# Sigmoid of the gated experts through the hyperbolic tangent, in a two-layer transformer kernel on one core

## The reference

```python
def _forward(x, ...):
    x1 = jnp.einsum('btd,hd->bth', x, sw1) + sb1
    x2 = jnp.einsum('btd,hd->bth', x, sw2) + sb2
    sh = _ln(jax.nn.silu(x1) * x2, s_ln_g, s_ln_b)            # every token
    shared_out = jnp.einsum('bth,dh->btd', sh, sw3) + sb3
    ...
    h1 = jnp.einsum('md,ehd->meh', x_moe, ew1) + eb1
    h2 = jnp.einsum('md,ehd->meh', x_moe, ew2) + eb2
    z = _ln(jax.nn.silu(h1) * h2, sel_ln_g, sel_ln_b)         # 512 chosen tokens
    out_all = jnp.einsum('meh,edh->med', z, ew3) + eb3
    ...
```

## Time and profile before

| | before |
|---|---|
| median of 3 runs | 1099.81 us (1099.57 to 1100.39) |
| the profiled execution, its own time | 1103.98 us |
| its span in the trace | 1101.8 us |
| busy: PE, DVE, ACT, POOL | 810.7, 722.0, 367.8, 383.9 us |
| TensorE clock granted, mean of the span | 0.91 of full speed |
| chain that ended last, by engine | PE 34%, DVE 29%, issue 13%, ACT 9%, POOL 9% |

### The profile page before, as it was taken

One profiled execution on the slowest core, in us unless ns is written; L12 is line 12 of the kernel. 1 busy time (PEld: TensorE's weight loads), 2 busy tenths in 40 slices (PEclk: granted clock), 3 DMA queues, 4 the chain that ended last, 5 costly groups with the idle time before them and its releaser, 6 DMA issues.

```text
span 1101.8 us, 27848 instructions
## 1 busy us (share of the span) xinstructions
PE 810.7 (74%) x10046; PEld 567.4 (51%) x10047; DVE 722.0 (66%) x1986; ACT 367.8 (33%) x752; POOL 383.9 (35%) x642
## 2 busy tenths in 40 slices
PE   2455527888898888988898888885777777773486
PEld 2344326556666655665666666563444454442364
DVE  4799764565766667565665656664767676675566
ACT  3333313333342433424243342532232423321110
POOL 3566421424233332433324243332232323313322
PEclk9986558999999999999999999997999999995588
DMA  5644300000000000000000000003121211111200
GB/s 214 229 161 170 126 1 1 3 0 0 0 0 0 0 0 0 0 0 0 0 0 0 0 0 1 11 15 97 32 63 32 64 32 64 41 50 39 78 1 5
DMA packets 22250, 42.17 MB, mean 38 GB/s; under 512 B 3341, under 2 KB 17815, under 8 KB 21321
## 3 DMA queue, kind: packets, MB, share of 16 engines
q1 hardware_dynamic: 21512, 40.01, 10.9%
q0 software_dynamic: 704, 1.71, 0.5%
HBM read 33.19 MB, written 8.91 MB: 38 GB/s over the span
## 4 chain that ended last, share of the span: by engine, by line
PE 34%; DVE 29%; issue 13%; ACT 9%; POOL 9%; DMA 2%; POOLq 2%; SPq 0%; DVEq 0%; ACTq 0%
DVE mx L1261 8%; PE ps L385 7%; POOL rs L1625 3%; PE ps L552 3%; PE ps L535 3%; DVE hl L1303 2%; PE ps L594 2%; PE ps L391 2%; PE ps L590 2%; PE ps L589 2%; ACT pT L907 2%; ACT hh L847 2%; PE ps L483 1%; PE ps L587 1%; PE ps L392 1%
## 5 line engine op out<-in xcount | busy, mean ns | idle before, releaser
L1623 POOL TENSOR_TENSOR rs<-mv,cst 128x1 f32<-128x1 f32 x164 | 35.8, 219 | 589.5 <-DVE mv L1061 529.4
L1261 DVE TENSOR_REDUCE mx<-ps 128x16 f32<-128x2048 f32 x48 | 109.4, 2280 | 0.0
L847 ACT CAST xh<-ps 128x256 bf16<-128x256 f32 x48 | 17.9, 372 | 264.7 <-PE ps L385 264.7
L1625 POOL TENSOR_TENSOR rs<-rs,cst 128x1 f32<-128x1 f32 x164 | 90.8, 554 | 12.8
L907 ACT ACTIVATE pT<-ps 128x1024 f32<-128x1024 f32 x96 | 93.4, 1030 | 2.1 <-PE ps L535 2.1
L391 PE MATMUL ps<-w_hi,hh 128*128 (+1 forms) x272 | 74.8, 275 | 7.5 <-DVE hl L1303 5.7
L552 PE MATMUL ps<-pT,v 128*32 128x128 f32 x1536 | 58.1, 285 | 24.1 <-ACT pT L907 24.1
L535 PE MATMUL ps<-qh,khm 32*128 32x128 bf16 x768 | 45.0, 222 | 41.8 <-issue 34.6
L847 ACT COPY mT<-ps 128x128 bf16<-128x128 bf16 x48 | 12.8, 266 | 187.7 <-PE ps L514 187.7
L392 PE MATMUL ps<-w_hi,hl 128*128 (+1 forms) x272 | 74.6, 274 | 0.0
L393 PE MATMUL ps<-w_lo,hh 128*128 (+1 forms) x272 | 74.6, 274 | 0.0
(11 more groups left out here) (338 smaller groups left out, 2675.4 us busy)
## 6 DMA issues: line engine op xcount, KB each, us to landing
stage<-in_w SPq DMA_DIRECT2D x16, 768.0 KB, 5.2
vec<-in_vec SPq DMA_DIRECT2D x4, 1152.0 KB, 7.6
vec<-in_tw SPq DMA_DIRECT2D x16, 216.0 KB, 2.6
ctxc<-in_ctx SPq DMA_DIRECT2D x20, 128.0 KB, 2.3
comb<-x SPq DMA_DIRECT2D x16, 128.0 KB, 2.1
comb<-t SPq DMA_DIRECT2D x16, 128.0 KB, 2.0
shared<-x1b SPq DMA_DIRECT2D x16, 128.0 KB, 1.7
out<-x SPq DMA_DIRECT2D x16, 128.0 KB, 1.8
```

The lines of the kernel that those rows point to most:

```text
L847: return nc.scalar.copy(dst, src)
L1261: nc.vector.tensor_reduce(mx[:, :], att.rearrange("p g s k -> p (g s) k"), AX.X, ALU.max, negate=True).then_inc(m_max, 1)
L1625: tt(rs[:, i, :], rs[:, i, :], halves, ALU.pow).then_inc(done, 1)
```

## The change

In both places where silu is computed, ACT applies Tanh to half of the argument in place of Exp to its negative, and DVE computes (tanh + 1) * a with one scalar_tensor_tensor in place of an addition, a reciprocal and a product. The factor 0.5 that is then missing goes into the product with the other half of the hidden tile, which becomes a scalar_tensor_tensor as well. (sigmoid(a) = (tanh(a/2) + 1)/2.) Two semaphores (`s_e1`, `s_r`) and two waits per block go with the operations.

```diff
             def sh_e(f):
                 act.wait_ge(s_hb, f + C1)
-                A(de[:, 0:HM], h[:, 0:HM], ACT.Exp, scale=-1.0).then_inc(s_e, 1)
+                A(de[:, 0:HM], h[:, 0:HM], ACT.Tanh, scale=0.5).then_inc(s_e, 1)
...
             def hidden_exp(t):
...
-                A(de[:, HM * (t % 2):HM * (t % 2) + HM], ps[:, t % 2, 0:HM], ACT.Exp, scale=-1.0).then_inc(d_e, 1)
+                A(de[:, HM * (t % 2):HM * (t % 2) + HM], ps[:, t % 2, 0:HM], ACT.Tanh, scale=0.5).then_inc(d_e, 1)
...
             def sh_gated(f):
                 dve.wait_ge(s_e, f + C1)
-                ts(de[:, HM:2 * HM], de[:, 0:HM], 1.0, None, ALU.add).then_inc(s_e1, 1)
-                dve.wait_ge(s_e1, f + C1)
-                nc.vector.reciprocal(de[:, 0:HM], de[:, HM:2 * HM]).then_inc(s_r, 1)
-                dve.wait_ge(s_r, f + C1)
-                tt(h[:, 2 * HM:3 * HM], h[:, 0:HM], de[:, 0:HM], ALU.mult).then_inc(s_a, 1)
+                stt(h[:, 2 * HM:3 * HM], de[:, 0:HM], 1.0, h[:, 0:HM], ALU.add, ALU.mult).then_inc(s_a, 1)
                 dve.wait_ge(s_a, f + C1)
-                tt(h[:, 3 * HM:4 * HM], h[:, 2 * HM:3 * HM], h[:, HM:2 * HM], ALU.mult).then_inc(s_g, 1)
+                stt(h[:, 3 * HM:4 * HM], h[:, 2 * HM:3 * HM], 0.5, h[:, HM:2 * HM], ALU.mult, ALU.mult).then_inc(s_g, 1)
...
             def gated(t):
...
-                link(ts(h[:, 0:HM], de[:, HM * (t % 2):HM * (t % 2) + HM], 1.0, None, ALU.add))
-                link(nc.vector.reciprocal(h[:, HM:2 * HM], h[:, 0:HM]))
-                link(tt(h[:, 0:HM], h12[:, 0:HM], h[:, HM:2 * HM], ALU.mult))
-                link(tt(h[:, 2 * HM:3 * HM], h[:, 0:HM], h12[:, HM:2 * HM], ALU.mult))
+                link(stt(h[:, 0:HM], de[:, HM * (t % 2):HM * (t % 2) + HM], 1.0, h12[:, 0:HM], ALU.add, ALU.mult))
+                link(stt(h[:, 2 * HM:3 * HM], h[:, 0:HM], 0.5, h12[:, HM:2 * HM], ALU.mult, ALU.mult))
```

## The result

The changed kernel takes **1083.99 us** (median of 4 runs, 1082.29 to 1084.76), the kernel before 1100.1 in the same comparison: 16.1 us less. The ratio, worked out over the single runs, is 0.9847, 95% interval 0.9826 to 0.9867, which is 16.8 us. Forecast were 1085.4 us and a gain of 14.4. A second comparison, with more runs, gave 1083.57 us after 1102.25 (18.7 us less) and a ratio of 0.984 (0.9822 to 0.9857), which is 17.6 us.

What follows compares the result with a forecast made beforehand. The prediction took stage C for a loop of waits, bound by no engine. Gains of 9.5 (blocks 1 to 13), 2.4 (blocks 14 and 15) and 2.5 (final stage), 14.4 us off 1099.8, gave 1085.4 us, range 1082 to 1088.

Steps and rivals of the forecast that it cites:

- the room of 0.74 us a block: Stage C: PE's projections let t1's transposes start at most 0.74 us earlier a block, of 1.22 saved on DVE.
- Rival A: Stage C: PE's projections don't hold the transposes, so all 1.22 us a block pass on; 20.8 us less, 1079.0; chance 7%.
- rival B: Stage C, blocks 1 to 13: another wait of nearly the same length leaves no gain; only 4.9 us, 1094.9; chance 7%.
- the gain of blocks 1 to 13: Stage C: twelve blocks gain 0.74 us each and block 1 gains 0.59, together 9.5 us.
- I count no change: PE's clock: low stretches counted as unchanged, with 2 us more to 5 us less to be expected.
- rival C: PE's clock in stage C and final stage turns beyond the forecast, likely in favour: 19.4 us less, 1080.4; chance 14%.
- Price of the two operations: DVE: the two new scalar_tensor_tensor cost 0.33 us each with the hand-over, 0.66 together; upper end 0.76.
- Blocks 14 and 15: End of stage C: no projections stand in the way, so both pass on all 1.22 us, 2.4 us together.
- Final stage: Gated operations of tiles 0 and 3 gain 1.25 and 1.23 us, 2.5 together; tiles 1 and 2 nothing.
- Tanh for Exp at nothing: ACT: Tanh takes as long as Exp and comes from the same loaded table, so no change.
- Rival D: ACT: Tanh is not in the loaded table, so loads are added; 24 us slower, 1123; chance 4%.
- The cost of profiling: The profiled execution's 4.2 us above the runs' median were taken as profiling cost; the gain was taken off the median.

Runs made afterwards that it cites:

- one_more: The changed kernel with one more scalar_tensor_tensor of 128x128 on DVE in stage C's shared layer, its result unused: 1082.72 us, ratio 0.9832.
- root_first: The changed kernel with the attention's root ahead of the gated one on POOL, and sh_sum behind sh_y on DVE: 1082.1 us, ratio 0.9828.
- v_behind: The changed kernel with projection_v moved behind the transposes of t1 on PE: 1077.83 us, ratio 0.9795.
- before_again: The kernel before, unchanged, run once more for a second trace: 1101.44 us, ratio 1.0002.
- t1_first_old_ops: The kernel before with the attention's root first on POOL, sh_sum behind sh_y on DVE, t1's transposes ahead of both projections on PE: 1077.96 us, ratio 0.978.

## Why the prediction was right, and where it was not

- *The bound, and the room of 0.74 us a block*: right to the hundredth up to the transposes, and so are the 0.59 of block 1 (8.28 us from `maxima` to the transposes before, 7.69 after). `one_more` (nothing lost), `root_first` (nothing gained) and `v_behind` (0.45 gained) show that PE's order holds them now. Rival A (1079.0) is excluded by the 16.53 us, rival B (1094.9) too.
- *The term that was mis-sized* is the gain of blocks 1 to 13: 12.4 us for 9.5. Of the 2.9, 13 x 0.06 = 0.8 came from behind the start of the transposes, where xh follows 0.07 us sooner when they needn't wait. The rest is the step "I count no change" on the clock: three low stretches, 2.15 us (2.0 in the prediction, which counts block 1 from 17.33 and not from 17.18), went, and went in every trace. The prediction had these 2 us inside its range, as a part of what might come, and gave rival C, which takes the final stage along, 14%; its reason (PE has shorter gaps) fits the traces. The stage C part of C happened, the final stage's part in some executions only, and C's 1080.4 as a whole did not.
- *Price of the two operations*: 0.63 us with their hand-overs in stage C, 0.66 forecast, and 0.66 in the final stage (1035.16 to 1035.82). The first is shorter than the tensor_tensor (0.260 for 0.292), which I had excluded on the ground that both stream the same two inputs; it made no difference in blocks 1 to 13.
- *Blocks 14 and 15*: 2.5 for 2.4. *Final stage*: 2.4 for 2.5 in the first trace. Two amounts of the clock nearly cancel in it: 0.2 less from hidden 2 to out 0, and 0.25 more from out 3 to the last operation of DVE (6.55 for 6.30).
- *Tanh for Exp at nothing*: right, 310 ns each. Rival D was a real danger of a neighbouring choice: Sigmoid itself costs 26 us more. Its price was too high, 34 us, as one of the two loads falls into ACT's wait.
- *The cost of profiling*: not confirmed. The 4.2 us by which the profiled execution lay above the median were a spread between executions: the changed kernel's profiled one took 1084.13 us, inside its own 1082.29 to 1084.76, and that of `before_again` 1100.58 with a median of 1101.44. As the gain was taken off the median, the forecast doesn't rest on it.
- *The sum*: 12 x 0.80 + 0.65 = 10.25, with 2.15 (clock) + 2.5 + 2.4 = 17.3 us, against 16.8 and 17.6 by the ratios of the two comparisons (16.1 and 18.7 by the medians). That the forecast of 14.4 came so near the first median is in part luck: the clock went the favourable way by 2.15 us, and the runs scatter by as much.

## What to carry to other kernels

Before an engine's saving is summed over its instructions, look at the instruction in which its path joins another engine's order: what can be had is the time between the earliest start that its own engine allows and its start (0.74 of 1.22 us here, where the profile showed 0.58 of idle time), and what stands in front of it in program order is the next thing to move. Moving three calls to other places in their engines' orders was worth more than 40 operations fewer, 20 of them reciprocals (23 to 24 us against 16 to 18, each alone in the kernel before), and together they gave 44. A function that replaces others should come from the table that is loaded anyway: Tanh cost nothing, Sigmoid 26 us more.

## What the hardware showed that I had not expected

- A short wait of PE can go with more than its own length: with 0.58 us of it ahead of 0.45 us of transposes and another 1.48 us of waiting, three or four of 13 blocks had a stretch at 1.2 GHz, at 0.4 to 1.0 us each; without it there was none in seven traces of six kernels. Where PE had time to spare, such a stretch cost nothing (15.94 us in `t1_first_old_ops`).
- A table load is carried out ahead of the wait of the activation it belongs to, so that it hides in ACT's idle time; where there is none it costs 1.41 us, of which 1.28 are the load.
- A scalar_tensor_tensor of 128x128 that adds a constant and multiplies took 0.260 us in stage C and 0.286 in the final stage, where the tensor_tensor took 0.292 in both; the one with two products took 0.292.
- DVE's `y_of` on 128x256 took 0.40 to 0.41 us where POOL's operation was nearly over as it began, and 0.57 to 1.27 beside it, ending 0.13 to 0.16 us behind it each time. An operation that came later on POOL so went with a longer one on DVE, for which the profile shows no wait.
